# An attention and feed-forward layer on one core: x read by channel, values stored with 16 columns a head, the first row of maxima loaded earlier

## The reference, cut to what matters

```
q = x @ q_w.T + q_b
xd = conv(x over the sequence, 3 taps per channel, stride 2, padding 1) + conv_b     # 1024 positions
k = xd @ k_w.T + k_b;  v = xd @ v_w.T + v_b
out = softmax(q k^T / 4) v, per head;  x = layernorm(x + out @ out_w.T + out_b)
x = layernorm(x + x + 0.5 * (silu(layernorm'(x) @ w1 + b1) @ w2 + b2))               # w1, w2 dequantised
```

## Time and profile before

| | us |
|---|---|
| median of 3 runs (lowest, highest) | 4122.21 (4111.5, 4124.09) |
| the profiled execution's own time | 4118.34 |
| its span | 4116.5 |
| stage project, from the first load of x to the first matmul of attention | 32.0 to 298.7 |
| stage attention, to its last matmul | 298.7 to 3046 |
| busy over the span: PE, DVE, ACT, POOL | 95%, 86%, 68%, 21% |
| DMA, share of the 16 engines' span | 24.7% |

### The profile page before, as it was taken

How to read it: one execution, slowest core, us unless ns; L and a number is a source line. 1 busy time by engine, 2 the same in 40 slices (tenths; PEclk the granted TensorE clock), 3 DMA queues, 4 the chain that set the end, 5 groups by cost and what they waited for, 6 DMA issues and landing times. The chain is left out here.

```text
span 4116.5 us, 78021 instructions
## 1 busy us (share of the span) xinstructions
PE 3901.7 (95%) x22952; PEld 2042.5 (50%) x22952; DVE 3559.5 (86%) x4373; ACT 2781.8 (68%) x5283; POOL 867.2 (21%) x535
## 2 busy tenths in 40 slices
PE   7988999999999999999999999999968999899898
PEld 5653333333333333333333333333326887778777
DVE  6658999999999999999999999999948999989996
ACT  3436888888888888888888888888744444444444
POOL 5430000000000000000000000000006777767774
PEclk9998999999999999999999999999978999999999
DMA  7992113004113211311411311221121122122210
GB/s 253 338 307 55 33 34 82 30 29 82 32 32 64 52 30 41 71 32 32 83 32 32 64 45 32 53 62 32 36 65 53 62 67 76 62 61 68 75 61 26
DMA packets 217885, 286.39 MB, mean 70 GB/s; under 512 B 25521, under 2 KB 127921, under 8 KB 217778
## 3 DMA queue, kind: packets, MB, share of 16 engines
q1 hardware_dynamic: 217778, 285.33, 24.7%
HBM read 165.69 MB, written 118.49 MB: 69 GB/s over the span
## 5 line engine op out<-in xcount | busy, mean ns | idle before, releaser
L685 DVE TENSOR_REDUCE half_max<-first_ps 128x2 f32<-128x1024 f32 x2048 | 2413.4, 1221 | 262.6 <-PE first_ps L579 258.6
L660 ACT ACTIVATE probs<-score_ps 128x512 f32<-128x512 f32 x4096 | 2114.8, 603 | 561.5 <-PE score_ps L604 561.5
L604 PE MATMUL score_ps<-q_s,k_s 49*128 49x512 f32 x4096 | 1435.1, 474 | 22.8 <-DMA q_s<-max_row 7.0
L604 PEld LDWEIGHTS score_ps<-q_s,k_s 49*128 49x128 f32 x4096 | 569.6, 184 | 1279.5 <-ACT probs L660 1179.3
L614 PE MATMUL pv_ps<-probs,v_s 128*32 128x512 f32 x8192 | 1094.2, 606 | 0.0
L579 PE MATMUL first_ps<-k_s,q_s 48*128 48x512 f32 x4096 | 905.3, 421 | 20.9 <-PEq L639 12.9
L1052 POOL TENSOR_TENSOR num<-num,rden 128x1024 f32<-128x1024 f32 x32 | 86.7, 2710 | 2775.5 <-DMA rden<-rden_d 2775.5
L902 ACT ACTIVATE tanh<-fc_ps,b_half 128x512 f32<-128x512 f32 x256 | 175.2, 685 | 472.6 <-PE fc_ps L857 467.9
L579 PEld LDWEIGHTS first_ps<-k_s,q_s 48*128 48x128 f32 x4096 | 402.5, 187 | 73.6 <-DVE half_max L685 18.6
L1033 POOL TENSOR_TENSOR a_lo<-act_f,a_hi 128x512 fp32r<-128x512 f32 x256 | 375.3, 1466 | 173.2 <-DVE a_hi L985 173.2
L980 DVE SCALAR_TENSOR_TENSOR act_f<-tanh,y 128x512 f32<-128x512 f32 x256 | 298.6, 1166 | 56.3 <-ACT y L904 55.8
(11 more groups left out here) (85 smaller groups left out, 2754.7 us busy)
## 6 DMA issues: line engine op xcount, KB each, us to landing
q_s<-q_hi_d SPq DMA_DIRECT2D x512, 64.0 KB, 2.1
o_d<-o_sb SPq DMA_DIRECT2D x128, 256.0 KB, 2.0
x_in<-x_in SPq DMA_DIRECT2D x32, 512.0 KB, 4.9
q_hi_d<-q_hi SPq DMA_DIRECT2D x32, 512.0 KB, 3.1
q_lo_d<-q_lo SPq DMA_DIRECT2D x32, 512.0 KB, 3.9
v_d<-v_f SPq DMA_DIRECT2D x32, 512.0 KB, 4.3
k_s<-k_hi_d SPq DMA_DIRECT2D x128, 128.0 KB, 4.2
v_s<-v_d SPq DMA_DIRECT2D x32, 512.0 KB, 6.5
```

Source lines behind the costliest of these rows:

```text
L604: pe.matmul(bank(s, u)[:, :], k_s[g][at, a, t * P:(t + 1) * P], q_s[g][at, a, :], start=True, stop=True).then_inc(scored, 1)
L660: nc.scalar.activation(probs[s % 2][:, u, :], bank(s, u)[:, :], ACT.Exp).then_inc(exped, 1)
L685: dve.reduce_max(half_max[g % 2][:, :, a * TT + t, keys], first_ps[keys][:, :, :], AX.X)\
```

## The change

x is given to the kernel a second time, laid out by channel, and project loads it straight into `x_t`: the transposes, the copies out of PSUM and the left edge column of `x_t` go, and the PSUM space that comes free makes `q_ps`, `k_ps` and `v_ps` double. The convolution starts with the tap that needs no neighbour, and its first column is an instruction of its own for each channel chunk (L418 or L420 of the changed kernel), which reads the last column of the block before from the other `x_t` buffer. `v_d` holds, for each partition and group, 16 columns a head without the ones; the ones are set once in the resident tiles `v_s` by four memsets on VectorE, and the load of the values writes 16 of every 32 columns. The first `load_max` stands behind the loads of group 1 and no longer behind those of group 3.

```diff
-    v_d = scratch("v_d", [B, NK, H * VC])
+    v_d = scratch("v_d", [B, P, G, KT * HG * D])
+    x_cols = x_c.rearrange("b (c p) n -> b p c n", p=P)
...
-    vs = e["v_d"][b].rearrange("(t p) c -> p t c", p=P)[:, :, g * HG * VC:(g + 1) * HG * VC]
-    sp.dma_start(e["v_s"][g][:, :, :, :].rearrange("p t h c -> p t (h c)"), vs).then_inc(e["kv_loaded"][g], 16)
+    vs = e["v_d"][b][:, g, :].rearrange("p (a d) -> p a d", d=D)
+    sp.dma_start(e["v_s"][g][:, :, :, :].rearrange("p t h c -> p (t h) c")[:, :, 0:D], vs).then_inc(e["kv_loaded"][g], 16)
...
-                sp.dma_start(x_in[j][:, :, :], x_blk[BPB * b + j]).then_inc(x_loaded[j], 16)
+                sp.dma_start(x_t[j][:, :, :], x_cols[b][:, :, j * QB:(j + 1) * QB]).then_inc(x_loaded[j], 16)
...
-                sp.dma_start(by_row(v_d[b][keys, :]), v_f[i][:, :, :, :].rearrange("p t h c -> p t (h c)"))\
-                    .then_inc(stored[i], 16)
+                tiles = slice(j * KB // P * HG * D, (j + 1) * KB // P * HG * D)
+                sp.dma_start(v_d[b][:, :, tiles], v_f[i][:, :, :, :].rearrange("p g t x -> p g (t x)")).then_inc(stored[i], 16)
...
-                    sp.wait_ge(turned, CC * (BPB * b + j + 1))
+                    m = BPB * b + j
+
+                    sp.wait_ge(q_mm, 1 + CC * m + 2 * CC)
+                    sp.wait_ge(begun, 1)
+                    sp.wait_ge(conv_up, 1 + CU * m + (2 * CU if j + 1 < BPB else CU))
...
-                        last = pe.transpose(xt_ps[c][:, t * P:(t + 1) * P], x_in[j % BPB][:, t, c * P:(c + 1) * P],
-                                            ident[:, :])
...
-                    nc.scalar.activation(x_t[i][:, c, 1:QB + 1], xt_ps[c][:, :], ACT.Copy).then_inc(xt_up, 1)
...
+                    if j == 0:
+                        dve.tensor_copy(conv[i][:, c, 0:1], acc[1][:, c, 0:1]).then_inc(conv_up, 1)
+                    else:
+                        dve.scalar_tensor_tensor(out=conv[i][:, c, 0:1], in0=x_t[j - 1][:, c, QB - 1:QB],
+                                                 scalar=w(c, 0), in1=acc[1][:, c, 0:1], op0=ALU.mult, op1=ALU.add)\
+                            .then_inc(conv_up, 1)
...
+            for g in range(G):
+                dve.memset(v_s[g][:, :, :, :], 1.0).then_inc(ones_up, 1)
...
-                pool.memset(v_f[i][:, :, :, :], 1.0).then_inc(ones_up, 1)
...
             for g in groups[1:]:
                 load_kv(sp, e, 0, g)
                 load_q(sp, e, 0, g)
-            load_max(0, 0)
+                if g == 1:
+                    load_max(0, 0)
```

More of the change, by code:

```diff
@@ L52, with build_layer @@
 NROWS = S2_R + FC * C
-def build_layer(nc, x, wq_t, wk_t, wv_t, wo_t, w1_q, w2_q, cols, rows, out):
+def build_layer(nc, x, x_c, wq_t, wk_t, wv_t, wo_t, w1_q, w2_q, cols, rows, out):
     x_blk = x.rearrange("(n t p) c -> n p t c", t=TT, p=P)
@@ L254, in project @@
 def project(nc, e):
-    x_blk, col, ident, wq, wk, wv, qb_scaled = (
-        e[k] for k in ("x_blk", "col", "ident", "wq", "wk", "wv", "qb_scaled"))
+    x_cols, col, wq, wk, wv, qb_scaled, v_s = (e[k] for k in ("x_cols", "col", "wq", "wk", "wv", "qb_scaled", "v_s"))
     q_hi_d, q_lo_d, k_hi_d, k_lo_d, v_d = (e[k] for k in ("q_hi_d", "q_lo_d", "k_hi_d", "k_lo_d", "v_d"))
@@ L260, in project @@
         two = range(2)
-        x_in = [sb(f"x_in{j}", [P, TT, C]) for j in range(BPB)]
-        x_t = [sb(f"x_t{i}", [P, CC, QB + 1]) for i in two]
+        x_t = [sb(f"x_t{j}", [P, CC, QB]) for j in range(BPB)]
         conv = [sb(f"conv{i}", [P, CC, KB]) for i in two]
@@ L270, in project @@
         k_lo = [sb(f"k_lo{i}", [P, CC, KB], F32R) for i in two]
[L271 to L274, removed]
+        v_f = [sb(f"v_f{i}", [P, G, KB // P, HG * D]) for i in two]
+        q_ps = [[ps(f"q_ps{i}_{c}", [P, QB]) for c in range(CC)] for i in two]
+        k_ps = [ps(f"k_ps{i}", [P, CC, KB]) for i in two]
+        v_ps = [ps(f"v_ps{i}", [P, KB // P, C]) for i in two]
         x_loaded = [sem(f"x_loaded{j}") for j in range(BPB)]
         stored = [sem(f"stored{i}") for i in two]
-        turned, xt_up, edge_up, acc_up, conv_up = (sem(n) for n in ("turned", "xt_up", "edge_up", "acc_up", "conv_up"))
+        acc_up, conv_up = sem("acc_up"), sem("conv_up")
         q_mm, k_mm, v_mm = sem("q_mm"), sem("k_mm"), sem("v_mm")
@@ L282, in project, with each_block @@
         ST = 5 * 16
+        CU = 2 * CC
         block = ctx.enter_context(nc.Block())
-        def each_block(eng, start, end):
+        def each_block(eng, body):
             with eng.Fori(0, B - 1) as b:
                 for j in range(BPB):
-                    start(b, j + 1)
-                    end(b, j)
+                    body(b, j)
             for j in range(BPB):
-                if j + 1 < BPB:
-                    start(B - 1, j + 1)
-                end(B - 1, j)
+                body(B - 1, j)
         @block.sync
@@ L333, in _ @@
                 sp.wait_ge(stored[i], 1 + ST * BPB // 2)
+            sp.wait_ge(ones_up, G)
             load_kv(sp, e, 0, 0)
@@ L342, in _ @@
         def _(pe):
[L343 to L352 removed]
             def products(b, j):
                 m, i = BPB * b + j, j % 2
[L357 removed]
+                pe.wait_ge(x_loaded[j], 16 * (b + 1))
                 for h in range(CC):
```

83 lines of the change are left out of this document (34 added, 49 removed).

## The result

| | before | after |
|---|---|---|
| median of 5 runs (lowest, highest), us | 4121.86 (4111.50, 4124.09) | 4097.50 (4091.81, 4099.08) |
| the profiled execution | 4118.34 | 4098.69 |

The ratio of the runs is 0.994, with a 95% interval of 0.9926 to 0.9954: 24 us less, where 34 were forecast (4122 against the 4088 of the prediction).

A forecast was written before the change was run, and what follows sets the result against it. TensorE was taken to set project's period, DMA close behind, with transfers deciding its end. Gains 22.7 + 3.4 + 1.5 + 5.5 = 33.1, less 1 for exposed small-piece loads, gave 32 us: forecast 4088, overall range 4075 to 4155.

The forecast's parts named there:

- Part 1: In project, removing the transposes shortens TensorE's block period from 7.77 to 6.93 us, gaining 22.7 us over 27 periods.
- Rival (b): Project becomes bound by transfers: period falls only to 7.3 us, gain 12.7 instead of 22.7, time 4098; chance 0.13.
- The landing that does not grow: In project, value stores still land 4.3 us after issue late in the stage, so DMA keeps up with TensorE's period.
- Part 2: At project's first block, query products start when x lands, without transposes first; gain 3.4 us (2.4 to 3.4).
- Part 3: At the end of project, four stores of 0.26 MB less shorten the transfers; gain taken as 1.5 us.
- the slack at `stored`: In project, the margin between a value store's landing and its buffer's reuse, expected to shrink from 3.0 to 1.3 us.
- Part 4: At attention's start, the row of maxima issued behind group 1 lets scores start earlier; gain 5.5 us (3 to 6.1).
- Rival (c): At attention's start, group 3 holds up group 1's row of maxima: 6 us less gain, time 4094; chance 0.15.
- the three sets take 11 us each: At attention's start, three sets of loads spanned 298.7 to 331.9, so groups 2 and 3 arrive near 333.5 and 344.5.
- Part 5: In attention, 28 value loads in 64 B pieces take 3.2 to 4.1 us each, hidden within their slack: no loss.
- the slack of 2.2 us: In attention, how much longer a value load may last before TensorE's score waits for the row of maxima.
- rival (a): In attention, the value load outlasts its slack, paid 28 times; time 4157 at 26 ns a piece, 4191 at 30.7; chance 0.32.

The follow-up runs named there:

- x_only: Kernel before with only x laid out by channel (values stored as before, first row of maxima behind group 3): 4106.31 us, ratio 0.9964 to before.
- changed_again: The changed kernel itself, unedited, run once more on another chip: 4094.85 us against 4124.60 for the kernel before, ratio 0.9933.
- store_twice: Changed kernel with each block's value store issued a second time into a spare tensor nobody reads: 4116.64 us, ratio 0.9979 to before.
- max_only: Kernel before with only the first row of maxima issued behind group 1: 4119.16 us, ratio 0.9987 to before.
- v_32B: Changed kernel with each value load cut into two transfers of 32 B pieces: 4206.82 us, ratio 1.0202 to before.
- v_only: Kernel before with only the values stored with 16 columns a head and loaded in 64 B pieces: 4131.52 us, ratio 1.002 to before.

## Why the prediction was right, and what was off

The sign and the range held, and the mechanisms of the gains were right. The size was 32 us by the sum; 24 were measured, and 28 with the clock's scatter at the end taken out. (The sum and the 3.9 us that the median lay above the profiled execution give 4090; the forecast of 4088 is 2 us lower without a reason.) Step by step:

- **Part 1 (27 periods x 0.84 = 22.7 us)**: 22.1 by block 27. The period is 6.89 and not 6.93, which gives 23.8, but the first block takes 1.6 us longer than that period (its query products take 5.24 us and not 3.60). Rival (b) did not come about in the changed kernel; x_only, with 11% more bytes, comes near it in its last blocks (7.22 us, where the rival has 7.3). "The landing that does not grow" was a weak argument against it: the value store lands 5.0 us after its issue now, where it took 4.3. And "VectorE has 2 us a block to spare" was wrong: VectorE is busy 172 of 200 us, see the last section. It cost nothing.
- **Part 2 (3.4)**: 2.7. The memsets (0.91 us each) are over 0.4 us before the first product, and x itself landed at 36.2 and not 35.5.
- **Part 3 (a gain of 1.5)**: this is the step that failed. The stretch from block 27 to attention got 1.4 us longer (0.3 in `changed_again`), though its four stores are smaller. I costed those stores by their bytes and left the rest of the end as it was. But when the period falls to 6.89, the slack at `stored` is used up (0.27 us at 159.95 and 8.37 at 258.02), so that bytes left over from the whole stage come out there; store_twice and x_only show how much. And the loads of q behind the first value load held SyncE 6.7 us and not 1.0, ahead of those four stores, where the sum had 1 us for all small pieces in the open; what this hold cost is not isolated. Parts 1 to 3 together gave 23.4 where my sum had 27.6.
- **Part 4 (5.5)**: 6.3 with the whole wait of the earlier trace rows gone; max_only alone gives 5. Rival (c), that group 3 holds up the next row, isn't seen here, with 2.9 us of waits in all attention; with pieces of 32 B it came about, once, with 7.1 us. The reading that the three sets take 11 us each was off: in the kernel before they are issued from 298.8 on at 6.1 us each, and the row behind them at 322.0.
- **Part 5 (no loss in the slack, 1 us in the open)**: the mechanism was right. The prediction had a price by rate (16.1 ns by the straight line) and one by the packets' own time (12.4 ns of `col`). Like for like, a 64 B piece took 12.0 ns by rate and 15.6 ns of its own time, so both near rows came within a third. The load became 0.65 us longer, less than the 1.2 to 2.1 predicted, and v_32B puts the slack of 2.2 us at 2.6. The attention between the first score and the last `first` lost 2.9 us; the waits for the row are the only part of it that the trace names. The Trainium skill, page "DMA: Bandwidth & Descriptors", Specifications, puts the least piece for the full rate at 512 B and says that the engines read, modify and write below it. It gives no price, and the 30.7 ns a piece that the prediction put beside it in rival (a) are not seen: 12.0 ns at 64 B in this direction, from DRAM to SBUF. That such pieces miss the full rate is seen, with 85 GB/s against the 267 of the earlier trace rows. Its section "Why small descriptors are slow (HBM only)", a fixed charge a piece, agrees in kind: a piece with an eighth of the bytes of the earlier trace rows takes 12.0 ns and not an eighth of 30.7.
- That rival (a) would cost each microsecond 28 times was right in v_32B, and too low: a microsecond of wait cost 1.7.

That the time came out inside the range is no luck: each gain is seen at its place. The range was wide, though, and the forecast inside it was high by the end of project and by the clock.

Open: what SyncE's hold of 6.7 us at the end of project costs, why the first query products take 5.24 us, and why the rate of the transfers in project rises from 338 to 364 GB/s with x by channel.

## What to carry to other kernels

When one engine and the transfers are both above 95% in a stage, work out the period that each would set and expect the longer one, and look at the end of the stage too, where what the slower side has left over comes out. A DMA share of 0.99 is not proof that the rate can't rise: it was 337 GB/s with that share and 364 when the engine asked for more. Test the two savings apart: here fewer bytes alone gave nothing, the shorter period alone 16 us, both 23. Small pieces may be cheap, but price them by the list that they stand in: here a load of 4096 pieces was nearly free with some 2.2 us of slack, and each microsecond beyond came 28 times, because the row of maxima queued behind it. Before a difference of a quarter per cent is explained from one pair of traces, look where the clock falls in each, and give both versions the same cover.

## What the runs showed of the hardware

- **Filling TensorE can shorten a stretch.** 4 matmuls a step that nobody reads took 8 to 9 us off the kernel before and 7 to 10 off the changed one; the granted clock stayed at 1.00, where it had been 0.50.
- **The clock fell behind some short waits and not behind others**: 0.57 over 4 us after the 1.71 us of 662.79 (v_32B); behind the 2.23 us of 614.24 it stayed at 1.00.
- **VectorE stands while GpSimd works.** In project of x_only the two convolution instructions that start beside GpSimd's subtraction take 3.73 us together, and end when GpSimd's two are done; the next ones, 0.87 for two:

```profile
164.87 0.42 DVE L430 CAST k_hi<-k_f 128x512 fp32r<-128x512 f32 x1
165.03 2.47 POOL L451 TENSOR_TENSOR q_lo<-q_f,q_hi 128x1024 fp32r<-128x1024 f32 x1 [2.96 <-DVE q_hi L428]
165.20 3.73 DVE L406 TENSOR_SCALAR acc<-x_t,col 128x256 f32<-128x256 f32 x2
167.46 1.32 POOL L454 TENSOR_TENSOR k_lo<-k_f,k_hi 128x512 fp32r<-128x512 f32 x1
168.85 0.87 DVE L410 SCALAR_TENSOR_TENSOR acc<-x_t,col,acc 128x256 f32<-128x256 f32 x2
```

 In the changed kernel the cast of k meets it too: 2.11 us in the mean from 60 to 260, 0.42 where it stands clear (1.60 in the kernel before). GpSimd's subtraction is hardly longer (2.47 us here, 2.35 in the mean of the changed kernel). The Trainium skill, "Trainium Architecture — The Big Picture", section "What this means for kernel authors", calls the port that these two share an exclusive lock; the rows agree, in that VectorE's 3.73 us end 0.15 us behind GpSimd's second instruction.
- **Many pieces hold the engine that issues them, or the transfers behind them.** The two value loads of 4096 pieces each took SyncE 5.8 us to issue in v_32B. One took 0.40 in the changed kernel, but where SyncE did not wait for it to land, the next two loads of q took 6.73 us to issue (242.62). Behind a first value load of 64 B pieces these took 5.95 to 6.73 us (v_only, store_twice, changed), behind one of 512 B pieces 1.04 and 1.05 (before, x_only).
- **DMA engines with a full share do not always move the same.** From 60 to 240 us, at a DMA share of 1.00 to 1.05, the 16 engines moved 338 GB/s before, 364 in x_only, 341 in the changed kernel and 352 in store_twice.
